# Norms of a streamed x: one product with a block matrix of ones, root and reciprocal in the PSUM bank

## The reference, cut to what matters

```
xn = transpose(x, (2, 0, 1))                       # node, item, row
x_norm = xn / max(norm(xn, over rows), 1e-12)      # one norm per node and item
mean_sim = einsum('nbl,mbl->nm', x_norm, x_norm) / B
# then: top 30% of each row of mean_sim -> graph A, degrees, normalised An
# x <- layernorm(x + An^T (x W) + bias)
# x <- layernorm(x + second graph layer(x))
```

## Time and profile before

| | |
|---|---|
| median of 3 executions | 1126.88 us (1126.37 to 1128.78) |
| the profiled execution | 1131.65 us |
| its span in the profile | 1129.9 us |
| mean granted clock of PE | 0.968 |
| busy share PE, DVE, ACT, POOL | 86%, 70%, 45%, 21% |
| reciprocals of the first stage, first and last start | 16.87 us and 112.42 us |
| last product of rows_01 starts | 127.51 us |

### The profile page before, as it was taken

One profiled execution on the slowest core, in us unless ns is written; L12 is line 12 of the kernel. 1 busy time (PEld: TensorE's weight loads), 2 busy tenths in 40 slices (PEclk: granted clock), 3 DMA queues, 4 the chain that ended last, 5 costly groups with the idle time before them and its releaser, 6 DMA issues. The chain is left out here.

```text
span 1129.9 us, 18915 instructions
## 1 busy us (share of the span) xinstructions
PE 971.3 (86%) x7052; PEld 569.8 (50%) x7052; DVE 787.3 (70%) x1659; ACT 506.2 (45%) x847; POOL 241.2 (21%) x295
## 2 busy tenths in 40 slices
PE   2999957768989898989898898989898989898995
PEld 2666754534545454545545454545454545454552
DVE  5999469844767675758584849494949484858576
ACT  4675446354534353535353535253535343444431
POOL 2566234212202111111111111112020202020301
PEclk9999987778999999999999999999999999999998
DMA  5441310010102020202020111102020202020010
GB/s 225 153 180 58 132 38 1 1 38 1 38 1 76 1 75 0 74 0 74 1 73 14 60 30 44 50 24 74 0 74 0 74 0 74 0 74 37 0 38 37
DMA packets 21967, 55.00 MB, mean 49 GB/s; under 512 B 1328, under 2 KB 1456, under 8 KB 19888
## 3 DMA queue, kind: packets, MB, share of 16 engines
q1 hardware_dynamic: 21936, 54.60, 13.9%
HBM read 37.82 MB, written 16.78 MB: 48 GB/s over the span
## 5 line engine op out<-in xcount | busy, mean ns | idle before, releaser
L240 PE MATMUL bank<-arena 128*128 128x512 f16 (+2 forms) x1456 | 446.9, 325 | 19.6 <-DVE arena L1506 9.1
L241 PE MATMUL bank<-arena 128*128 128x512 f16 (+2 forms) x1456 | 445.7, 324 | 0.0
L242 PE MATMUL bank<-arena 128*128 128x512 f16 (+2 forms) x1456 | 444.0, 323 | 0.0
L240 PEld LDWEIGHTS bank<-arena 128*128 128x128 f16 x1456 | 143.0, 98 | 131.2 <-issue 17.2
L242 PEld LDWEIGHTS bank<-arena 128*128 128x128 f16 x1456 | 143.4, 98 | 112.0 <-issue 5.1
L241 PEld LDWEIGHTS bank<-arena 128*128 128x128 f16 x1456 | 143.4, 98 | 95.8 <-issue 3.0
L392 POOL TENSOR_TENSOR arena<-arena 128x512 f32<-128x512 f32 x64 | 80.9, 1264 | 514.5 <-ACT arena L874 514.5
L1370 DVE BATCH_NORM_STATS2 stats<-arena 128x6 f32<-128x512 f32 x64 | 44.4, 694 | 145.5 <-POOL arena L392 145.5
L945 ACT ACTIVATE arena<-bank 128x512 f16<-128x512 f32 x128 | 76.3, 597 | 146.5 <-PE bank L242 144.9
L1413 DVE SCALAR_TENSOR_TENSOR arena<-bank,arena 128x512 f16<-128x512 f32 x128 | 84.4, 686 | 59.5 <-ACT arena L945 59.5
L874 ACT ACTIVATE arena<-bank,bias_c,col 128x512 f32<-128x512 f32 x64 | 49.7, 777 | 118.6 <-PE bank L242 118.6
(11 more groups left out here) (266 smaller groups left out, 1526.5 us busy)
## 6 DMA issues: line engine op xcount, KB each, us to landing
arena<-in_x SPq DMA_DIRECT2D x32, 1024.0 KB, 6.1
out_dram<-arena SPq DMA_DIRECT2D x15, 1024.0 KB, 8.1
arena<-in_w_lang_t SPq DMA_DIRECT2D x1, 1024.0 KB, 5.3
arena<-in_w_grav_t SPq DMA_DIRECT2D x1, 1024.0 KB, 9.0
arena<-in_w_v SPq DMA_DIRECT2D x1, 1024.0 KB, 5.5
arena<-in_w_o_t SPq DMA_DIRECT2D x1, 1024.0 KB, 7.7
out_dram<-arena SPq DMA_DIRECT2D x4, 256.0 KB, 2.4
adj_sb<-in_adj SPq DMA_DIRECT2D x1, 64.0 KB, 14.3
```

The lines of the kernel that those rows point to most:

```text
L240: pe.matmul(dst, ah, bh, start=start, stop=False)
L241: pe.matmul(dst, ah, bl, start=False, stop=False)
L242: return pe.matmul(dst, al, bh, start=False, stop=stop)
```

## The change

Instead of bringing the sums onto 128x16 numbers and back, the kernel keeps one number per partition and node, 128x512, all the way:

- `same_item` (128 by 128, ones where two partitions hold the same item) takes the place of `item_of`. One float32 product (`norms`, 512 columns) sums over the item's partitions and leaves the sum in each of them, in bank 5 or 6. `item_sums`, `spread`, `repeat` and `squared_norms` are gone.
- The root (ACT, with the factor X_HAT in its scale) and the reciprocal (DVE) work in that bank, in place, on 128x512. The bound 1e-12 moves: tiny sums are lifted to `LEAST`, and `normalise` bounds the reciprocal above with a minimum.
- ACT makes the squares in two instructions of 1024 elements: rows 0 and 1 into SBUF, rows 2 and 3 into PSUM banks 2 and 3 (`pair23`).
- DVE sums the four rows by three instructions of 512 elements: two additions, each with one operand in PSUM, and a scalar_tensor_tensor whose accumulator gives `chunk_sum` in place of `chunk_max`; X_UP is lowered by 2^3 to suit.
- Orders: DVE inverse_norms(c), normalise(c), sum_squares(c+2). ACT high(c), root(c+1), square(c+3). PE: norms(c+3) between the halves of rows_01(c).

```diff
@@ -59,7 +59,10 @@
     X_HAT = 2.0 ** 12
     S_SCALE = 1.0 / (X_HAT * X_HAT * B)
-    X_UP, W_UP, A_UP, H_UP, K_UP = 2.0 ** 13, 2.0 ** 14, 2.0 ** 12, 2.0 ** 8, 2.0 ** 14
+
+    LEAST = 1e-30
+
+    X_UP, W_UP, A_UP, H_UP, K_UP = 2.0 ** 10, 2.0 ** 14, 2.0 ** 12, 2.0 ** 8, 2.0 ** 14
     XW_DOWN, U_DOWN, VO_DOWN, V_DOWN = 2.0 ** -17, 2.0 ** -16, 2.0 ** -22, 2.0 ** -16
     M_DOWN, HALF_DOWN = 2.0 ** -16, 2.0 ** -13
     ALPHA = 1.0 / (X_UP * W_UP * XW_DOWN * A_UP)
...
@@ -82,7 +85,10 @@
         def sem(name):
             return ctx.enter_context(nc.semaphore(name))
-        bank = [ctx.enter_context(nc.psum_tensor(f"bank{i}", [P, 512], F32)) for i in range(8)]
+        bank01 = [ctx.enter_context(nc.psum_tensor(f"bank{i}", [P, 512], F32)) for i in range(2)]
+        pair23 = ctx.enter_context(nc.psum_tensor("pair23", [P, 2, 512], F32))
+        bank = bank01 + [pair23[:, i, :] for i in range(2)]
+        bank += [ctx.enter_context(nc.psum_tensor(f"bank{i}", [P, 512], F32)) for i in range(4, 8)]
         cross_ps = [bank[4][:, 0:P], bank[1][:, 3 * P:4 * P], bank[2][:, 2 * P:3 * P], bank[3][:, P:2 * P]]
...
@@ -166,7 +170,7 @@
         xn_h = at(0, [TILES, NODES], F16)
         xn_l = at(64 * KIB, [TILES, NODES], F16)
         xc = [at(k * KIB, [CL, NODES]) for k in (128, 136, 144, 152, 176, 184)]
-        sq = [at(k * KIB, [CL, NODES]) for k in (160, 168)]
+        sq = [at(k * KIB, [CL // 2, NODES]) for k in (160, 164)]
         S = at(176 * KIB, [KB, NODES])
         work = at(184 * KIB, [KB, NODES + 8])
         ssum = [at((193 + 2 * i) * KIB - KIB // 2, [NODES]) for i in range(2)]
...
@@ -323,11 +327,11 @@
             pool.wait_ge(s["rank_made"], 1)
             pool.tensor_copy(rank[:], rank_i[:]).then_inc(s["rank_made"], 1)
-            pool.affine_select(out=item_of[:], in_=item_of[:], compare_op=ALU.is_ge, fill=0.0, base=0,
-                               pattern=[[-LG, CB]], channel_multiplier=1).then_inc(cs, 1)
+            pool.affine_select(out=same_item[:], in_=same_item[:], compare_op=ALU.is_ge, fill=0.0, base=0,
+                               pattern=[[-LG, CB], [0, LG]], channel_multiplier=1).then_inc(cs, 1)
             pool.wait_ge(cs, 9)
-            pool.affine_select(out=item_of[:], in_=item_of[:], compare_op=ALU.is_ge, fill=0.0, base=LG - 1,
-                               pattern=[[LG, CB]], channel_multiplier=-1).then_inc(s["consts_made"], 1)
+            pool.affine_select(out=same_item[:], in_=same_item[:], compare_op=ALU.is_ge, fill=0.0, base=LG - 1,
+                               pattern=[[LG, CB], [0, LG]], channel_multiplier=-1).then_inc(s["consts_made"], 1)
             pool.affine_select(out=ident_up[:], in_=ident_up[:], compare_op=ALU.not_equal, fill=1.0 / HALF_DOWN,
                                base=0, pattern=[[-1, P]], channel_multiplier=1).then_inc(s["picks_made"], 1)
...
@@ -431,23 +435,12 @@
             pe.wait_ge(s["consts_made"], 3)
             pe.wait_ge(s["picks_made"], 3)
-            def item_sums(c, slot):
+            def norms(c, slot):
                 pe.wait_ge(s["ssum_ready"], c + 1)
-                wait(pe, s["nrm_in"], c)
-                for k in range(KB):
-                    mm = pe.matmul(bank[7][:, k * CB:(k + 1) * CB], ssum[slot][:, k * P:(k + 1) * P], item_of[:],
-                                   start=True, stop=True)
-                mm.then_inc(s["nrm_ps"], 1)
-
-            def spread(c, slot):
-
-                pe.wait_ge(s["rinv_ready"], c + 1)
                 wait(pe, s["xn_ready"], c - 1)
-                for k in range(KB):
-                    mm = pe.transpose(bank[5 + slot][:, k * P:(k + 1) * P],
-                                      rinv_rep[:, k, :], ident[:])
-                mm.then_inc(s["spread_ps"], 1)
+                pe.matmul(bank[5 + slot][:], same_item[:].rearrange("p b g -> p (b g)"), ssum[slot], start=True,
+                          stop=True).then_inc(s["nrm_ps"], 1)
             def cross_product(r, xh, xl, start, stop):
                 mine = slice(r * P, (r + 1) * P)
...
@@ -491,20 +484,16 @@
             def rows_01(c, slot, first=False, last=False):
-                if not isinstance(c, int) or c + 2 < NC:
-                    spread(c + 2, slot)
                 pe.wait_ge(s["xn_l_ready"], c + 1)
                 gram(c, (0, 1), first=first, ts=range(0, CL // 2))
                 if not isinstance(c, int) or c + 3 < NC:
-                    item_sums(c + 3, 1 - slot)
+                    norms(c + 3, 1 - slot)
                 gram(c, (0, 1), last=last, ts=range(CL // 2, CL))
-            item_sums(0, 0)
-            spread(0, 0)
-            item_sums(1, 1)
-            spread(1, 1)
-            item_sums(2, 0)
+            norms(0, 0)
+            norms(1, 1)
+            norms(2, 0)
             rows_01(0, 0, first=True)
             with pe.Fori(0, (NC - 4) // 2) as j:
                 for t in (1, 2):
...
@@ -756,19 +745,14 @@
             def square(c):
                 act.wait_ge(x_loaded[c % SLOTS], 16 * (c // SLOTS + 1))
                 wait(act, s["ssum_ready"], c - 1)
-                act.activation(sq[c % 2], xc[c % SLOTS], ACT.Square).then_inc(s["sq_ready"], 1)
+                act.activation(sq[c % 2], xc[c % SLOTS][:, 0:CL // 2, :], ACT.Square).then_inc(s["sq_low_ready"], 1)
+                wait(act, s["ssum_ready"], c)
+                act.activation(pair23[:], xc[c % SLOTS][:, CL // 2:, :], ACT.Square).then_inc(s["sq_ready"], 1)
             def root(c):
-                act.wait_ge(s["nrm_in"], c + 1)
-                act.activation(sqn[:], sqn[:], ACT.Sqrt).then_inc(s["nrm_ready"], 1)
-
-            def repeat(c):
-
-                act.wait_ge(s["rinv_made"], c + 1)
-                wait(act, s["spread_ps"], c)
-                act.activation(rinv_rep[:].rearrange("p k (b g) -> p (k b) g", b=CB),
-                               rinv[:].rearrange("p k b -> p (k b)").unsqueeze(2).broadcast_to([P, KB * CB, LG]),
-                               ACT.Copy).then_inc(s["rinv_ready"], 1)
+                act.wait_ge(s["nrm_ps"], c + 1)
+                norm = bank[5 + c % 2][:]
+                act.activation(norm, norm, ACT.Sqrt, scale=1.0 / (X_HAT * X_HAT)).then_inc(s["nrm_ready"], 1)
             def high(c):
...
@@ -778,13 +762,11 @@
             square(0)
             square(1)
             root(0)
-            repeat(0)
             square(2)
             for c in range(NC):
+                high(c)
                 if c + 1 < NC:
                     root(c + 1)
-                    repeat(c + 1)
-                high(c)
                 if c + 3 < NC:
                     square(c + 3)
...
@@ -1029,45 +1010,36 @@
         @block.vector
         def _(dve):
             def sum_squares(c):
+                dve.wait_ge(s["sq_low_ready"], c + 1)
                 dve.wait_ge(s["sq_ready"], c + 1)
+                dve.tensor_tensor(sq[c % 2][:, 0, :], pair23[:, 0, :], sq[c % 2][:, 0, :],
+                                  ALU.add).then_inc(s["half_summed"], 1)
+                dve.tensor_tensor(pair23[:, 1, :], pair23[:, 1, :], sq[c % 2][:, 1, :],
+                                  ALU.add).then_inc(s["half_summed"], 1)
+                dve.wait_ge(s["half_summed"], 2 * c + 2)
                 wait(dve, s["nrm_ps"], c - 1)
-                dve.tensor_reduce(ssum[c % 2], sq[c % 2].rearrange("p l n -> p n l"), AX.X,
-                                  ALU.add).then_inc(s["ssum_ready"], 1)
-
-            def squared_norms(c):
-
-                dve.wait_ge(s["nrm_ps"], c + 1)
-                wait(dve, s["rinv_made"], c)
-                dve.tensor_scalar(sqn[:].rearrange("p k b -> p (k b)"), bank[7][:, 0:KB * CB], NORM_EPS * NORM_EPS,
-                                  0.0, ALU.max, ALU.max, accum_out=chunk_max[:, c:c + 1]).then_inc(s["nrm_in"], 1)
+                dve.scalar_tensor_tensor(ssum[c % 2], pair23[:, 1, :], LEAST, sq[c % 2][:, 0, :], ALU.max, ALU.add,
+                                         accum_out=chunk_sum[:, c:c + 1]).then_inc(s["ssum_ready"], 1)
             def inverse_norms(c):
                 dve.wait_ge(s["nrm_ready"], c + 1)
-                wait(dve, s["rinv_ready"], c)
-                dve.reciprocal(rinv[:], sqn[:]).then_inc(s["rinv_made"], 1)
+                norm = bank[5 + c % 2][:]
+                dve.reciprocal(norm, norm).then_inc(s["rinv_made"], 1)
             def normalise(c):
-                dve.wait_ge(s["spread_ps"], c + 1)
-                dve.wait_ge(s["sq_ready"], c + 1)
-                dve.scalar_tensor_tensor(xc[c % SLOTS], xc[c % SLOTS], X_HAT,
-                                         bank[5 + c % 2][:].unsqueeze(1).broadcast_to([P, CL, NODES]),
-                                         ALU.mult, ALU.mult).then_inc(s["xn_ready"], 1)
+                dve.wait_ge(s["rinv_made"], c + 1)
+                dve.scalar_tensor_tensor(xc[c % SLOTS], bank[5 + c % 2][:].unsqueeze(1).broadcast_to([P, CL, NODES]),
```

(28 more changed lines are left out.)

## The result

The changed kernel takes 1152.6 us (median of 4, 1150.07 to 1154.17), against 1127.83 us for the kernel before (median of 4). The ratio is 1.0215, with a 95% interval of 1.0192 to 1.0239: some 25 us slower. The forecast was 1150.4 us, in a range of 1142 to 1168.

A forecast was written before the change was run, and what follows sets the result against it. DVE was taken to bound the kernel, then a chain of 8.07 us per chunk through reciprocal, multiplication, copy and root. Stage end +22.5 and PE's clock +1.0 gave +23.5 on 1126.88: 1150.4 us, range 1142 to 1168.

The forecast's parts named there:

- What bounds it: First stage: DVE sets the pace before, 6.15 of 6.43 us busy; afterwards a chain through ACT of 8.07 us per chunk.
- The reciprocal: DVE, 512 elements per partition: 154 ns fixed plus 6.1 ns per element, 3.28 us; bounds 0.69 and 4.76 us.
- The additions: DVE's sum of squares as three instructions of 512 elements: 2.1 us instead of 3.68, a gain of 1.6 per chunk.
- The chain: Per chunk: reciprocal, multiplication 2.28, ACT's copy 1.80, root 0.60, handovers 0.11; reciprocal plus 4.79, or 8.07 us.
- Start: First stage on DVE: first reciprocal at 13.0 us, 3.9 us sooner than 16.87.
- End: First stage's end: last multiplication to 139.7 us against 116.37, POOL to 145.8 against 123.31, +22.5.
- PE's clock: PE's last 4.15 us of the stage, after a pause of 3.9: half clock may cost 0 to 4.1 us; 1.0 taken.
- PE's load: PE per chunk in the first stage: falls to about 5.1 us, covered by DVE; the next floor if uncovered.
- The faster one: Rival: DVE's reciprocal at the pace of other work, 0.69 us; period 5.48, time 1107.8 us; chance 0.12.
- DVE's load alone: Rival: DVE's load of 7.7 us sets the period, needing the root before ACT's copy; 1144 us; chance 0.05.
- Half clock for the whole stage: Rival: PE at half clock for most of the stage, 10.2 us per chunk, up to 30 more, 1180; chance 0.04.
- The rest of the program: Sign of being wrong: a stage after the picks that differs by more than 2 us.

The follow-up runs named there:

- the kernel with the cheap operation: Changed kernel with DVE's reciprocal replaced by a tensor_scalar over the same 512 elements of the same bank (an approximation): 1108.72 us, ratio to before 0.9833.
- the nine kernels: The kernels before and after the change and seven follow-up kernels; the program after the first stage takes 1001.4 to 1006.6 us in their profiled executions.
- the kernel with the old sum: Changed kernel with one square of 2048 elements and one tensor_reduce instead of three instructions, without accumulator and LEAST: 1167.23 us, ratio to before 1.0348.

## Why the prediction was right

Point by point, by its own steps:

- **What bounds it.** DVE's load, and then the chain through ACT. Both are in the trace, and putting the root first turned the one into the other, 10 us apart.
- **The reciprocal.** 3.28 us were forecast and 3.37 measured. The slope was read from 8 to 16 elements, 6.1 to 6.25 ns, and the lower end was taken; the upper was exact. Over 16 instructions that is 1.4 us too little. The upper bound of 9.0 ns, from the step 4 to 8, was not borne out: small instructions on this engine do not lie on the line (the fit gives 182 ns for 4 elements, and 167 were seen). The estimate of 4.4 us, from the repeat count of 8 in the Trainium skill ("VectorE: DVE Perf Modes", section "Walkthrough: the 8-slice pipeline in each mode") and its clock, lies 1 us above. Taking the count of 8 for eight cycles per element was the prediction's own step; an estimate with the page's 0.96 GHz makes the measured 6.25 ns six cycles.
- **The additions.** 2.1 us forecast; 2.02 measured from the first one's start to the end of the accumulator's read, and 1.94 from start to start where the next instruction doesn't wait. The row with an accumulator on which the third was priced (0.74 us) was too dear: it took 0.69.
- **The chain.** r + 4.79: with 3.37, 8.16 against 8.15 measured. The load of DVE (7.7) was 7.54 to 7.62, and so the wait 0.53 instead of 0.4.
- **Start.** First reciprocal forecast at 13.0, seen at 12.96.
- **End.** The last multiplication ended at 140.96 instead of 139.7; the reciprocal's 1.4 account for all of it. POOL ended at 147.04 instead of 145.8.
- **PE's clock.** It fell where it was feared, and cost 0 instead of the 1.0 put in. The step that failed is "the last 4.15 us may so cost": it was the chunk before the last that ran slow, and the clock was full again before the last one began. This error and the one of the reciprocal nearly cancel, by luck, so PE's last product starts 23.6 us later (151.13 against 127.51) where 23.5 was forecast. The agreement of the sum is better than that of its terms. Of the 2.2 us between the forecast and the median, 0.95 lie in the median of the kernel before, 1126.88 then and 1127.83 with a fourth execution.
- **PE's load.** Given as 5.1, and it is about 5.0 when nothing else holds it.
- **The rivals.** The faster one was worked out at 1107.8, and the kernel with the cheap operation gave 1108.7: its mechanism was sound, its premise false. "DVE's load alone" was given 1144 and would need another order; with that order 1142.4 was measured. Half clock for the whole stage didn't come about: with pauses of 1.1 and 1.6 us per chunk the granted clock reads 1.00 in every window of 8 us from 10 to 130.
- **The half clock at the start.** The prediction read it from products (0.63 us at 30.03, 0.38 at 34.70). The windows of the kernel before read a granted clock of 1.00 over the same time (28 to 34), and those of the changed kernel do so from 24 to 28, where its first products take 0.63 as well. What makes the first chunk's products slow stays open, and these rows don't show how soon PE gets its clock back. No term of the sum rested on it, only the rival of half clock for most of the stage.
- **The rest of the program.** A difference of more than 2 us after the picks was to be a sign of being wrong. It is 2.2 us in the pair of profiled executions, within the 5 us by which this rest varies over the nine kernels, so it tells nothing either way.
- **Slips that changed nothing.** The reduction's 3684 ns for 2048 elements are 1.8 ns each and not about 1; it is the multiplication (2278 ns) that comes to 1.1. It is no rate of all reductions: the one of 512 neighbouring elements to a single one in the kernel with the old sum takes 675 ns. Sixteen elements cost 100 ns more than one, not 90. The chances add up to 1 only if the 0.05 of the load rival are part of the 0.71, and the terms with the lower r of 3.0 give about 1145, not 1143.

What the prediction did not see is how much the split sum was worth by itself: it is a gain of 15 us, which the reciprocal used up and more.

## What to carry to other kernels

Before a cheap operation on few numbers is moved to where there are many, look for its rows at several sizes and take the slope: 0.25 us for 16 elements said nothing until it stood beside 0.20 for 8. Where a long instruction is taken from between two steps of a chunk, look for what it covered, and put what the next chunk waits for ahead of what it does not. And of a change with several parts, time each alone: here one part was a gain that the sum of them hid.

## What was not expected of the hardware

- A reciprocal on DVE costs 157 ns and 6.25 ns per element, from 32 to 256 elements to within 1 ns, from a bank as from SBUF.
- ACT's logarithm and exponential in place on 512 elements of a bank take 0.58 us each, as its root does.
- Busy time of PE in a stretch with pauses overstates its floor: 5.86 us busy per chunk before, with two pauses in it, 5.38 us when it was held up by nothing.
